# Attention's low parts of the probabilities: from VectorE and GpSimd together to one VectorE instruction a group

## What is computed

```python
    xn = rms_norm(x, gamma)
    qkv = xn @ w_qkv
    ...
    q = q * scale
    sim = jnp.einsum('bhid,bhjd->bhij', q, k)
    attn = jax.nn.softmax(sim, axis=-1)
    out = jnp.einsum('bhij,bhjd->bhid', attn, v)
    out = jnp.transpose(out, (0, 2, 1, 3)).reshape(b, n, DIM_INNER)
    return out @ w_out
```

## Time and profile before

| what | before |
|---|---|
| median of 3 runs | 2309.75 us |
| lowest and highest | 2306.97 and 2312.76 us |
| span of the profiled execution | 2302.3 us |
| median less that span | 7.45 us |
| busy in that span: TensorE, VectorE, ScalarE, GpSimd | 93%, 78%, 69%, 44% |
| attention in it | about 670 to 2250 us |

### The profile page before, as it was taken

The page is one execution under the profiler, slowest core; times in us unless marked ns, Lnnn a source line. Parts: engine busy times, 40 slices in busy tenths (PEclk is TensorE's granted clock), DMA queues, the critical chain, the costliest instruction groups (busy, mean ns, idle before and its releaser), DMA issues.

```text
span 2302.3 us, 32776 instructions
## 1 busy us (share of the span) xinstructions
PE 2142.9 (93%) x9032; PEld 1504.7 (65%) x9032; DVE 1805.1 (78%) x2535; ACT 1587.2 (69%) x1898; POOL 1004.2 (44%) x636
## 2 busy tenths in 40 slices
PE   6999459998779999999999999999999999999997
PEld 4777237776647666666766666666666667666654
DVE  5888867886588888887888788788888878888555
ACT  4666426664427877777787777777777787777873
POOL 1000100003025566565565656556565655656672
PEclk7999769998679999999999999999999999999998
DMA  3210003110000000000000000000000000000000
GB/s 115 63 49 19 0 0 75 43 30 15 1 3 1 12 1 14 3 10 10 7 12 4 12 3 10 15 1 12 5 11 3 10 15 1 12 2 10 11 1 19
DMA packets 25125, 36.59 MB, mean 16 GB/s; under 512 B 11807, under 2 KB 14239, under 8 KB 23711
## 3 DMA queue, kind: packets, MB, share of 16 engines
q1 hardware_dynamic: 24958, 34.56, 5.8%
HBM read 32.99 MB, written 1.43 MB: 15 GB/s over the span
## 4 chain that ended last, share of the span: by engine, by line
PE 73%; DVE 13%; issue 7%; ACT 4%; POOL 2%; DVEq 0%; DMA 0%; ACTq 0%; POOLq 0%
PE ps L478 14%; PE ps L480 13%; PE ps L479 13%; PE ps L586 8%; PE ps L608 8%; PE ps L609 8%; DVE m_part L1219 2%; PE ps L460 2%; DVE p_l L1249 2%; POOL p_l L380 1%; ACT p_raw L926 1%; DVE m_part L1331 1%; DVE kb L1207 1%; PE ps L613 1%; PE ps L453 1%
## 5 line engine op out<-in xcount | busy, mean ns | idle before, releaser
L380 POOL TENSOR_TENSOR p_l<-p_raw,p_h 128x512 fp32r<-128x512 f32 (+1 forms) x512 | 836.9, 1635 | 651.3 <-ACT p_h L930 645.4
L1219 DVE TENSOR_REDUCE m_part<-ps 128x1 f32<-128x512 f32 x960 | 643.3, 685 | 191.0 <-PE ps L586 186.1
L926 ACT ACTIVATE p_raw<-ps 128x1024 f32<-128x1024 f32 x512 | 524.9, 1025 | 308.6 <-PE ps L609 283.6
L930 ACT ACTIVATE p_h<-p_raw 128x1024 fp32r<-128x1024 f32 x512 | 543.0, 1061 | 27.5
L1249 DVE TENSOR_TENSOR p_l<-p_raw,p_h 128x512 fp32r<-128x512 f32 x384 | 431.0, 1123 | 63.9 <-ACT p_h L930 49.8
L608 PE MATMUL ps<-qa,ka 128*128 128x512 f32 x1024 | 418.3, 408 | 7.4 <-DMA qb<-m_t 7.4
L478 PE MATMUL ps<-p_h,v_l 128*65 128x512 f32 x1024 | 404.4, 395 | 7.2 <-DVE p_l L1249 6.1
L609 PE MATMUL ps<-qb,kb 65*128 65x512 f32 x1024 | 407.5, 398 | 0.0
L479 PE MATMUL ps<-p_h,v_h 128*65 128x512 f32 x1024 | 402.6, 393 | 0.0
L480 PE MATMUL ps<-p_l,v_h 128*65 128x512 f32 x1024 | 402.4, 393 | 0.0
L586 PE MATMUL ps<-ka,qa 128*128 128x512 f32 x960 | 381.9, 405 | 8.0 <-DVE m_part L1219 5.6
(11 more groups left out here) (177 smaller groups left out, 2730.8 us busy)
## 6 DMA issues: line engine op xcount, KB each, us to landing
big<-g_scratch SPq DMA_DIRECT2D x64, 256.0 KB, 3.2
xnp<-r_scratch SPq DMA_DIRECT2D x15, 512.0 KB, 4.8
big<-in_w1T SPq DMA_DIRECT2D x1, 2048.0 KB, 9.0
big<-in_w2T SPq DMA_DIRECT2D x1, 2048.0 KB, 13.5
x<-in_xT SPq DMA_DIRECT2D x4, 256.0 KB, 3.6
qk_raw<-in_w_qkv SPq DMA_DIRECT2D x32, 32.0 KB, 1.9
out_xT<-x SPq DMA_DIRECT2D x4, 256.0 KB, 2.0
wv_raw<-in_w_qkv SPq DMA_DIRECT2D x8, 64.0 KB, 1.9
```

Of the source, the lines that this page charges most:

```text
L380: nc.gpsimd.tensor_tensor(p_l[:, g % 4, tiles, :], p_raw[:, g % 4, tiles, :], p_h[:, g % 4, tiles, :].bitcast(fp32), ALU.subtract).then_in ...
L926: af(p_raw[:, g % 4, :, :], ps[:, 2 * (g % 2):2 * (g % 2) + 2, :], ACT.Exp).then_inc(exp_done, 1)
L930: af(p_h[:, g % 4, :, :], p_raw[:, g % 4, :, :], ACT.Copy).then_inc(ph_done, 1)
L1219: nc.vector.tensor_reduce(m_part[:, ds(c, 1), it:it + 1].rearrange("p a t -> p (a t)"), ps[:, 4 + it % 2, :], AX.X, ALU.max).then_inc(s_ma ...
```

## The change

All 512 low parts of attention go to VectorE, as one instruction of 128x1024 per group, with one semaphore, `pl_done`. GpSimd keeps the low parts of v and the scaling, as well as its part of the feed-forward layers; its queue loses the places that these had between the low parts. The even head now has `low_v` first and then the four pieces of `scale`; the odd head has piece 0, then `low_v`, then the other pieces.

```diff
-POOL_GROUPS = (2, 4)
-SCALE_GROUP = 3
...
             if g < 0:
                 c, g = c - 1, g + GROUPS
-            own = GROUPS - len(POOL_GROUPS)
-            eng.wait_ge(pl_even, own * (NC * head + c) + sum(i not in POOL_GROUPS for i in range(g + 1)))
-            eng.wait_ge(pl_odd, GROUPS * (NC * head + c) + g + 1)
+            eng.wait_ge(pl_done, GROUPS * (NC * head + c) + g + 1)
...
-            def low_part(head, c, g, start):
-
-                n = GROUPS * (NC * head + c) + g
-                pool.wait_ge(ph_done, n + 1)
-                if not start or g >= 4:
-                    pool.wait_ge(pv_done, n - 3)
-                tiles = slice(0 if g in POOL_GROUPS else 1, 2)
-                nc.gpsimd.tensor_tensor(p_l[:, g % 4, tiles, :], p_raw[:, g % 4, tiles, :], p_h[:, g % 4, tiles, :].bitcast(fp32),
-                                        ALU.subtract).then_inc(pl_odd, 1)
...
             def window(pair, par, scale_before, project):
                 head = 2 * pair + par
-                for g in range(GROUPS):
-                    low_part(head, 0, g, first_of_all(pair, par))
-                    if par == 0 and (0, g) == V_SPLIT[0]:
-                        low_v(head + 1, 1, GROUPS * NC * head + g + 1)
...
+                if par == 0:
+                    low_v(head + 1, 1)
+                for q in range(NC):
+                    if q == 1 and par == 1 and project:
+                        low_v(head + 1, 0)
+                    if scale_before:
+                        scale(head - 1, 1 - par, q, NC * (pair - 1) + q + 1 if par == 1 and later else None)
...
             def low_part(head, c, g, start):

-                if g not in POOL_GROUPS:
-                    n = GROUPS * (NC * head + c) + g
-                    dve.wait_ge(ph_done, n + 1)
-                    if not start or g >= 4:
-                        dve.wait_ge(pv_done, n - 3)
-                    tt(p_l[:, g % 4, 0, :], p_raw[:, g % 4, 0, :], p_h[:, g % 4, 0, :].bitcast(fp32),
-                       ALU.subtract).then_inc(pl_even, 1)
+                n = GROUPS * (NC * head + c) + g
+                dve.wait_ge(ph_done, n + 1)
+                if not start or g >= 4:
+                    dve.wait_ge(pv_done, n - 3)
+                tt(p_l[:, g % 4, :, :], p_raw[:, g % 4, :, :], p_h[:, g % 4, :, :].bitcast(fp32),
+                   ALU.subtract).then_inc(pl_done, 1)
```

More of the change, by code:

```diff
@@ L190, in macaron_kernel @@
         m_ready, mt_ps, mt_done, m_loaded = sem("m_ready"), sem("mt_ps"), sem("mt_done"), sem("m_loaded")
-        st_ps, exp_done, ph_done, pl_even, pl_odd, pv_done = (
-            sem("st_ps"), sem("exp_done"), sem("ph_done"), sem("pl_even"), sem("pl_odd"), sem("pv_done"))
+        st_ps, exp_done, ph_done, pl_done, pv_done = (
+            sem("st_ps"), sem("exp_done"), sem("ph_done"), sem("pl_done"), sem("pv_done"))
         s_ps, s_max = sem("s_ps"), sem("s_max")
@@ L371, in quant_ffn, with low_v, scale @@
                                                 ALU.subtract).then_inc(f_lo, 1)
-            def low_part(head, c, g, start):
-                n = GROUPS * (NC * head + c) + g
-                pool.wait_ge(ph_done, n + 1)
-                if not start or g >= 4:
-                    pool.wait_ge(pv_done, n - 3)
-                tiles = slice(0 if g in POOL_GROUPS else 1, 2)
-                nc.gpsimd.tensor_tensor(p_l[:, g % 4, tiles, :], p_raw[:, g % 4, tiles, :], p_h[:, g % 4, tiles, :].bitcast(fp32),
-                                        ALU.subtract).then_inc(pl_odd, 1)
-            def low_v(head, par, low_parts):
+            def low_v(head, par):
                 pool.wait_ge(v_hi, head + 1)
-                pool.wait_ge(pl_odd, low_parts)
                 nc.gpsimd.tensor_tensor(v_l[:, par, :, 0:DH], v_raw[:, :, par * DH:par * DH + DH],
                                         v_h[:, par, :, 0:DH].bitcast(fp32), ALU.subtract).then_inc(v_lo, 1)
-            def scale(head, par, piece, low_parts, wait_out=None):
+                pool.wait_ge(v_lo, head + 1)
+            def scale(head, par, piece, wait_out=None):
                 rows = slice(par * DH, par * DH + DH)
```

## The result

| | before | with the change |
|---|---|---|
| median of 4 runs | 2311.07 us | 2336.88 us |
| lowest and highest | 2306.97, 2312.76 | 2330.45, 2341.02 |
| ratio, with its 95% interval | | 1.0111 (1.0090 to 1.0132) |
| span of the profiled execution | 2302.3 us | 2336.3 us |
| from the first `m_col` of a head to the fifteenth, by 14 | 99.15 us | 101.04 us |

The change makes the kernel 1.1% slower, 26 us. The last line of the table is the time of one head in the middle of attention; 14 heads of 1.89 us more are 26.5 us. The two profiled spans differ by 34 us, but 7 us of that lie ahead of attention (its first matmul starts at 670.1 and at 677.0 us), where the two programs are the same.

The account below looks back on a forecast made before the run. TensorE, busy 93%, was taken as the bound. Terms 0 + 0.5 + 0.8 + 0.5 - 0.4 = +1.4 us a pair, for 7 pairs +10 us, added to the median: 2320 us, range 2298 to 2343.

Parts of the forecast that it names:

- the third rival: VectorE becomes the bound of the last chunk: `m_col` slips 1.2 us a head, +27 in all, 2337 us; chance 0.17.
- The price, 1.22 us: Each 128x1024 subtraction on VectorE takes 1.22 us, interpolated; VectorE's busy time in heads 5 and 6 rises to about 186 us.
- Ordinary groups cost nothing: In ordinary groups VectorE needs 2.34 us against TensorE's 2.77, so the new low part costs nothing.
- GpSimd's unloading gives nothing: GpSimd's low parts come off an engine that TensorE hardly ever waits for, so their removal gains nothing.
- Group 3 of chunk 0, +0.8: A low part now stands ahead of three maxima; the third tile goes out about 0.4 us late, twice a pair.
- `low_v`, +0.5: `low_v` on GpSimd meets a low part in one head of two, delaying it 0 to 1.3 us, mostly caught up: +0.5 a pair.
- The last chunk, 0: Last chunk, twice a pair: TensorE gains up to 0.7 us early, all given back as a longer wait for `m_col`; net 0.
- Behind the branch, +0.5: Behind the loop's branch, once a pair: VectorE doing both halves adds 0.53 us to TensorE's wait for the low part.
- Chunk 0, group 6, -0.4: In the odd head, TensorE's wait in chunk 0's group 6 goes: -0.4 us a pair.
- the third rival's second estimate: If ten remaining GpSimd instructions a pair each shut out a low part: at least 1.8 us a pair more, 2333 us.

## Why the prediction was right, and where not

The forecast was slower, by 10 us, 2320; the measurement is 2336.9, inside the range (2298 to 2343), and of the size of the third rival (2337). By its steps:

- **The price, 1.22 us.** Right: median 1.216. The load of VectorE, about 186 us in two heads, is 184.6.
- **Ordinary groups cost nothing; GpSimd's unloading gives nothing.** Right: chunks 1 and 2 have no new wait but that for `low_v`.
- **Group 3 of chunk 0, +0.8.** Right in kind, measured +1.2 a pair. All four kernels that move the low part or the third maximum away have 0 there.
- **`low_v`, +0.5.** The step that was most wrong. I took it to meet a low part in one head of the two, at 0 to 1.3 us, mostly caught up. It meets one in both, holds it 1.83 and 0.84 us, and costs +1.56. Taking it out gives that back. In the odd head `low_v` now stands behind a piece of `scale`; in the three kernels where it stands ahead of `scale` again, that head has no wait there, or under 0.1 us. I priced the instruction, and not its new place in GpSimd's queue. The page that I cited, SBUF — State Buffer of the Trainium skill, section "SBUF: two separate sides", speaks of the whole instruction as shut out. These rows agree within 0.2 us: a low part that starts 0.24 us after `low_v` ends 1.1 us after it, where one by itself takes 1.22.
- **The last chunk, 0.** Of groups 0 to 5, I had gains of 0.7 us a head in groups 0 and 2; the profile has the waits of these two gone, as forecast, but others of about the same size in groups 1 and 5, so 0 in sum. Of groups 6 and 7 I had the gain given back at `m_col`; instead 0.4 us a head are lost, in group 6, at the bank of a maximum (I had looked for a wait of over 1 us at `m_col` itself). Measured +0.8 a pair. That the two more low parts are the cause is shown: without them group 6 waits 0.25.
- **Behind the branch, +0.5.** Measured +0.6 for the starts of both heads, so the size is right, but by luck. The wait for the low part, which I had growing, fell by about 0.6 us a pair, and the wait for the row of maxima, which I had at nothing, grew by 1.1: the row is copied out later after the turn, behind ScalarE's copies.
- **Chunk 0, group 6, -0.4.** Measured -0.6.

The sum of these is 3.7 us a pair where I had 1.4: `low_v` was mis-sized by 1.1, the last chunk by 0.8, group 3 by 0.4. (The 2333 us of the third rival's second estimate should be 2332, which changes nothing.) The third rival gave the right total by the wrong mechanism. It had 2.4 us a pair more in the last chunk, from a dearer instruction or pieces of `scale`; the instruction was not dearer, and two fifths of the loss were `low_v`'s. That VectorE is busy 91% of the time in heads 5 and 6 was no cause in itself: a kernel that leaves it 29 of 32 low parts, and 175 of 197 us busy, is as fast as any here.

## What to carry to other kernels

When two engines exclude each other, work cut in halves and started together can cost one of them nearly the whole (here VectorE 1.12 us for a half and 1.22 for the whole, while GpSimd's half took 1.35, near its bare 1.29): give them whole instructions at times when the other does something that does not collide. When work goes onto an engine with time to spare, look for the stretches where it has none (here 3 of 32 groups), and leave just those where they were. And a rare long instruction on the emptied engine has to be placed or cut again, since nothing in its queue holds it where it was harmless.

## What the runs showed of the hardware

- Two subtractions started 0.24 us apart on GpSimd and VectorE ran nearly one after the other: 3.05 us for one of 1.22 behind one of 2.21. With the long one cut in four, the other engine got in between, and none of its low parts there took over 1.59.
- A standstill of TensorE of 2.8 to 3.0 us between heads, at full clock before, was followed by a granted 0.50, with 0.2 us lost at each of 13 or 14 matmuls, in all four cases. Such a wait for a DMA cost about twice its length. Six standstills of 1.6 to 1.9 us had the same behind them for a shorter time, and most of that length had not.
- The same 8 KB row, by the same code, landed after 1.8 to 2.2 us, 3.1 to 3.7 us, or 4.5 to 4.6 us, with none, one or two packets of the instruction queue q8 in between (157 of 160 rows in ten traces). Which is the cause of which no run shows.
